# Tail of the second cross attention: one expert's low part, the bias rows' low part and the fourth weight load change their places

## The reference, cut to what matters

```python
x = x + tanh(g_xattn[1]) * xattn1(layernorm(x), ctx_1024, ...)    # 16 heads of 16
xs = layernorm(x).reshape(T, D)                                   # T = 800, D = 256
dist = sqrt(max(|xs|^2 + |centroid|^2 - 2 xs @ centroid.T, 1e-12))
w, sel = top_k(dist, 2); w = softmax(w)                           # 8 experts, 2 for each token
for e in range(8):
    h = silu(xs @ Wg[e] + bg[e]) * (xs @ W1[e] + b1[e])           # 684 hidden channels
    out = out + we[:, e:e+1] * (h @ W2[e] + b2[e])
x = x + tanh(g_ffn[1]) * out
```

## Time and profile before

| | us |
|---|---|
| median of three launches | 783.92 (783.83 to 784.07) |
| the profiled launch, its own time | 782.88 |
| span of the profiled launch | 781.1 |
| PE busy in it | 711.4 (91%) |
| DVE, ACT, POOL busy | 490.2, 379.0, 220.6 |

### The profile page before, as it was taken

The page is one execution under the profiler, slowest core; times in us unless marked ns, Lnnn a source line. Parts: engine busy times, 40 slices in busy tenths (PEclk is TensorE's granted clock), DMA queues, the critical chain, the costliest instruction groups (busy, mean ns, idle before and its releaser), DMA issues.

```text
span 781.1 us, 13394 instructions
## 1 busy us (share of the span) xinstructions
PE 711.4 (91%) x4735; PEld 596.4 (76%) x4735; DVE 490.2 (63%) x956; ACT 379.0 (49%) x820; POOL 220.6 (28%) x238
## 2 busy tenths in 40 slices
PE   6999999999989699998998999998993799999996
PEld 3578888889955588577995576676773699999995
DVE  3266666665328799466657667777777465666662
ACT  4513233323362289554434466565766165656561
POOL 0006765555400043600003411114000322334232
PEclk9999999999999899998999999999996699999999
DMA  6500000000072200000000878436052388999972
GB/s 231 233 1 21 20 20 20 20 1 1 1 293 100 79 3 1 1 1 1 0 11 33 179 175 193 116 98 183 25 213 85 111 299 279 331 298 325 302 217 60
DMA packets 31441, 89.45 MB, mean 115 GB/s; under 512 B 4201, under 2 KB 20841, under 8 KB 28049
## 3 DMA queue, kind: packets, MB, share of 16 engines
q1 hardware_dynamic: 27537, 83.36, 32.9%
q0 software_dynamic: 3840, 5.25, 3.3%
HBM read 74.74 MB, written 10.38 MB: 109 GB/s over the span
## 4 chain that ended last, share of the span: by engine, by line
PE 75%; DVE 14%; ACT 4%; issue 4%; DMA 3%; POOLq 0%; SPq 0%; DVEq 0%; ACTq 0%
PE PS L514 71%; DVE SM L2124 2%; PE PS L1096 2%; PE PS L685 1%; DMA XB<-token_rows,XROW 1%; DVE RB L1879 1%; DVE SM L1791 1%; DVE RQ L1881 1%; DVE PROD L1774 1%; PE PS L1066 1%; DVE KTHL L2086 1%; PE PS L913 1%; ACT SQ L1141 1%; DVE RW L1787 1%; ACT RO L1271 1%
## 5 line engine op out<-in xcount | busy, mean ns | idle before, releaser
L514 PE MATMUL PS<-CTXH,WKV0H 128*128 128x362 f32 x256 | 86.4, 338 | 3.8 <-DVE PROD L1774 3.2
L514 PE MATMUL PS<-CTXH,WKV0L 128*128 128x362 f32 x256 | 84.0, 328 | 0.0
L514 PE MATMUL PS<-CTXL,WKV0H 128*128 128x362 f32 x256 | 84.0, 328 | 0.0
L2124 DVE TENSOR_REDUCE SM<-PS 100x1 f32<-100x362 f32 x128 | 64.5, 529 | 30.5 <-PE PS L514 29.7
L1397 ACT ACTIVATE WK<-PS 120x400 f32<-120x400 f32 (+1 forms) x96 | 48.3, 508 | 39.9 <-PE PS L514 39.2
L1813 DVE TENSOR_TENSOR RW<-PS,RW 128x400 f32<-128x400 f32 x64 | 36.8, 574 | 47.4 <-ACT RW L1207 33.7
L1207 ACT COPY RW<-PS 128x361 f32<-128x361 f32 x64 | 29.6, 463 | 65.0 <-PE PS L514 52.5
L1670 POOL DMA_INDIRECT out<-YO,TROW x20 | 33.0, 1649 | 96.8 <-DMA out<-YO,TROW 69.5
L514 PEld LDWEIGHTS PS<-CTXH,WKV0H 128*128 128x128 f32 x256 | 48.1, 188 | 12.8 <-DVE PROD L1774 6.5
L514 PE MATMUL PS<-KST,QST 97*100 97x362 f32 x128 | 51.4, 412 | 5.4 <-DVE SM L2124 4.2
L514 PE MATMUL PS<-RB,HTT 114*128 114x256 f32 (+1 forms) x240 | 55.2, 379 | 0.6 <-ACT HTT L1509 0.6
(11 more groups left out here) (326 smaller groups left out, 1813.6 us busy)
## 6 DMA issues: line engine op xcount, KB each, us to landing
RB<-W SPq DMA_DIRECT2D x14, 1368.0 KB, 6.6
RB<-W SPq DMA_DIRECT2D x20, 768.0 KB
KST<-keys_by_head SPq DMA_DIRECT2D x24, 362.0 KB
RQ<-W SPq DMA_DIRECT2D x6, 1368.0 KB
keys_by_head<-KTHL SPq DMA_DIRECT2D x8, 724.0 KB, 3.6
CTX<-ctxT SPq DMA_DIRECT2D x16, 361.0 KB, 7.0
RB<-WK SPq DMA_DIRECT2D x16, 200.0 KB, 2.2
RW<-WGU SPq DMA_DIRECT2D x1, 2304.0 KB, 8.5
```

The lines of the kernel that those rows point to most:

```text
L514: return pe.matmul(out, lhsT, rhs, start=start, stop=stop)
L2124: dve.tensor_reduce(SM1[:, q % 2, j:j + 1], PS[0:S, i % 2, 0:KVE], AX_X, ALU.max, negate=True).then_inc(sem["c_maximum_found"], 1)
```

## The change

Four moves, none of which adds or removes an instruction of the engines or a transfer:

- DVE: `gu_low(0, 1)` goes from behind `route()` to a place behind `statistics(2)`, ahead of the wait for the last mix; `statistics(3)` and `statistics(4)` go ahead of that wait too.
- DVE: the bias rows' low part goes from behind `route()` into it, between WLOW and XROW, where DVE waits for the names' product.
- ACT: the bias rows' high part goes ahead of the square root.
- SP: `load_weights(3)` with its wait goes ahead of the rows' store and the residual's stores.

```diff
@@ sync
             load_down(0)
             load_down(1)
+            sp.wait_ge(sem["expert_weights_low_ready"], N0 + 2)
+            load_weights(3)
             sp.wait_ge(sem["rows_copied"], B)
             sp.dma_start(XROWS.rearrange("(b s) c -> s b c", s=S), ROWS[:, :, :]).then_inc(sem["rows_stored"], 16)
             sp.wait_ge(sem["c_aside_ready"], 2 + B)
...
-            sp.wait_ge(sem["expert_weights_low_ready"], N0 + 2)
-            load_weights(3)
@@ scalar
+            act.wait_ge(sem["moe1_small_loaded"], 64)
+            act.wait_ge(sem["zeros_set"], 7)
+            act.copy(BROWS[0:40, 0:2 * HID1], BRAW).then_inc(sem["bias_rows_ready"], 1)
             act.wait_ge(sem["router_scores_shifted"], 2)
             act.activation(FAR, pairs(TOPS), ACT.Sqrt).then_inc(sem["router_function_taken"], 1)
...
             act.preload_act_table_set("silu_and_others")
-            act.wait_ge(sem["moe1_small_loaded"], 64)
-            act.wait_ge(sem["zeros_set"], 7)
-            act.copy(BROWS[0:40, 0:2 * HID1], BRAW).then_inc(sem["bias_rows_ready"], 1)
@@ vector
             for b in (0, 1, 2):
                 statistics(b)
+            gu_low(0, 1)
+            for b in (3, 4):
+                statistics(b)
             dve.wait_ge(sem["c_heads_mixed"], 4 * B)
             place_sums(B - 1, sides(PS[:, 6, 0:4 * S]))
             pack_values(B - 1, sides(PS[:, 6, 0:4 * S]))
-            statistics(3)
             divide(B - 1)
-            for b in (4, 5, 6, 7):
+            for b in (5, 6, 7):
                 statistics(b)
...
                 link(dve.tensor_tensor(WLOW, WEIGHT, WHIGH[:, :], ALU.subtract))
+                dve.wait_ge(sem["bias_rows_ready"], 1)
+                dve.tensor_tensor(BROWS[32:40, :], BRAW[32:40], BROWS[32:40, :],
+                                  ALU.subtract).then_inc(sem["bias_rows_ready"], 1)
                 named = PS[:, 7, 64:64 + NBLK]
                 dve.wait_ge(sem["router_scores_summed"], 4)
...
             route()
-            gu_low(0, 1)
-            dve.wait_ge(sem["bias_rows_ready"], 1)
-            dve.tensor_tensor(BROWS[32:40, :], BRAW[32:40], BROWS[32:40, :],
-                              ALU.subtract).then_inc(sem["bias_rows_ready"], 1)
             tokens_low(0)
```

## The result

| | before | changed |
|---|---|---|
| median of three launches, us | 783.92 (783.83 to 784.07) | 777.34 (776.76 to 777.44) |
| ratio of the times | | 0.9918 (0.9891 to 0.9945) |
| the profiled launch, its own time | 782.88 | 777.34 |
| span of the profiled launch | 781.1 | 775.5 |

One launch of the kernel before, of the 98 on record, took 1,166 us at a mean clock of 0.56, and no figure here has it in. The rows that answer to those of before come first, then an account of where the time went.

A forecast was written before the change was run, and what follows sets the result against it. PE was taken to bound the kernel, idling 4.12 us for block 0's gather. The turn's 3.91 us plus edit 1's 0.79 made 4.70 us off 783.92: 779.2 us, own range 778.2 to 780.2, with cases 777.6 to 781.0.

The forecast's parts named there:

- Edit 1: DVE about the last mix: the second low half and two statistics fit into DVE's wait; gain 0.79 us, bounds 0.5 to 1.1.
- Edit 2: Bias rows' low part on DVE, between WLOW and XROW: shifts XROW and WEIGHED later, a loss of 0.2 us.
- Edit 3: Bias rows' high part on ACT, ahead of the square root: covered by the exponential's wait for DVE, cost nothing.
- Edit 4: Weights 3 on SP done near 590; block 0's gather lands before PE's product ends, the turn moving 3.91 us sooner.
- two readings: DVE's two-input subtraction holds up POOL's gather instruction (first), or making transfer descriptors is not held up by it (second).
- The sum at the turn: Turn of block 0's tokens on PE: 3.91 us plus edit 1's 0.79 us, 4.70 us sooner in all.
- Cases 2 and 4: Block 0's gather: 2: its 2.77 us are its own, 780.2 us, chance 0.18; 4: stores slow it, 783.3 us, 0.07.
- Case 3: PE's clock comes back earlier since PE works on without a gap: 1 us more gain, 778.2 us; chance 0.10.
- case 5: Slower: weights 3 ahead of the rows' store on SP delay that store and the gather, up to 785.8 us; chance 0.03.
- The clock: PE's half clock from the route into block 0: no change taken, though 2.1 us either way was possible; 1 us each side.

The follow-up runs named there:

- four buffers: The changed kernel with four YO buffers for the rows that go out, in place of two: median 779.30 us, ratio 0.9954.
- filler: The changed kernel with 58 unread products in PE's waits in the route: 779.34 us; with bias rows behind the route and four buffers as well: 777.10 us.

## Why the prediction was right and wrong

**Edit 1, forecast -0.79.** Right: -0.77 in the trace, and 0.72 the other way when the two statistics were put back.

**Edit 2, forecast +0.2.** The right sign, too small: +0.36 by the experiment. I had XROW behind BROWS at 603.30 to 603.41, so 0.12 to 0.23 us later, and let WEIGHED and PE's product shift by the same 0.2. In the trace BROWS put XROW 0.26 us later (15.75 us behind the statistics of batch 7, was 15.49), and WEIGHED another 0.13, which my sum had at nothing: 0.92 us after XROW, where it was 0.79.

**Edit 3, forecast 0.** Right. With the bias rows' low part put back, the only other edit in the route, XROW stands 19.31 - 3.79 = 15.52 us behind the statistics of batch 7, where it was 15.49 before.

**Edit 4, the turn 3.91 sooner, loss of edit 2 included.** Right in its parts. Weights 3 had moved but for the last 1% by 587, which is 588.4 in the old trace's times, where I had them done near 590; that only adds cover. The instruction took 1.39 us, by my working 604.66 + 1.0 - 604.46 = 1.2. The landing took at most 2.08, I had 2.0. PE's product became late next, as said. From the slot weights' product to the turn it is 3.44 us, where it was 7.73: I had counted the 3.60 us of that product in full, but the turn follows 0.16 us ahead of its modelled end.

The Trainium skill (SBUF — State Buffer, Who interferes with whom) left two readings. The runs side with the first: 2.77 and 2.76 us with GUL behind WEIGHED, 1.39 and 1.27 with only the last 0.32 and 0.2 us of WEIGHED beside its start. They don't show it to hold for every such subtraction: BROWS has two inputs in SBUF too, ran beside the gather from 601.38 on in the kernel with the bias rows put back, and held nothing up.

**The sum at the turn.** Forecast -4.70, measured -4.67, and the same distance (24.44) in four profiles, one of them with four buffers. That it fits to 0.03 us is luck: the slot weights' product began 0.38 us sooner where 0.59 were forecast, and the turn followed it 0.18 us sooner than forecast, so two errors of 0.2 us cancelled. Cases 2 and 4 are refuted by the kernels above. Case 3 came true in part in this launch (0.58 of its 1 us). The store that case 5 delays was issued at 592.37, 5 us after the engines had gone quiet, so it didn't occur.

**The step that failed** is "The clock": "I take no change ... and keep 1 us to each side for the range", and with it the last step, from the profiled launch to the median by a fixed 1.04 us. I had looked for the clock's part only in block 0, where it gave 0.58 us, within my 1 us and the way case 3 has it. But PE's clock falls to a half at places all over the span, and these differ from launch to launch: at 543 us before and not after, for 20 us at 349 in the second launch of before. Of the 6.6 us, 4.67 are the forecast sum; the 1.42 us from ahead of the mix and the 1.04 us between profiled launch and median, less 0.49 us given back behind the turn, are the rest, which the forecast had at nothing. A fit over 201 launches of 11 kernels, each with its own level and the time at half clock worked out from the mean clock, gives 0.42 us (+- 0.01) of time for each us at half clock. The last mix, which no kernel here changed, stood anywhere from 580.8 to 589.6 us. Pooled over three chips, 97 launches of before have a median of 783.7 us (8 in 10 of them from 781.8 to 786.0), and 17 of the changed kernel 778.9 (776.5 to 782.5): a difference of 4.9 us, near the forecast 4.7, with 3.8 to 6.5 as its interval by redrawing the launches. The traces say the same: from the last mix to the end of the span it took 197.97 and 198.72 us in the two of before, and 193.79, 193.13 and 193.53 in the three of the changed kernel, 4.9 us less in the mean. If three of each are drawn at random, their medians differ by over 6.3 us, which is out of my range, in 22 draws of 100; 8 in 10 give 2.9 to 7.2. The range was 3.4 us wide and should have been about 4.3 for this alone.

The failure was in the range, then, not in the mechanism. That the launches shown of before agreed within 0.24 us had made its median look far firmer than it is; the page of before had the warning in the 1.04 us between profiled launch and median, which I took for a constant.

**Open.** Why blocks come late in some launches (0 to 1.6 us in all) and whether four buffers end that, what decides where the clock falls in a launch, and why WEIGHED came 0.13 us later behind XROW.

## What to carry to other kernels

When work is moved beside an indirect gather, ask three things of the trace in turn: does its POOL instruction start beside a long subtraction on DVE, what else is in the DMA engines until it lands, and what does its reader do meanwhile; here one moved line gave 4.30 us of the 4.67 at the turn. Work put into a wait costs by how far it runs past the wait's end, and it becomes the wait as soon as what was waited for gets faster. Compare two launches by distances from an event that the edit can't reach, and take the scatter of whole launches from a dozen, not from three that agree.

## What the runs showed of the hardware

- The first gather's instruction ended 1.07 to 1.09 us behind the DVE instruction that ran beside its start, whichever that was: behind GUL before (605.95 to 607.03) and with weights 3 held (604.79 to 605.86), behind WEIGHED in the changed kernel (602.66 to 603.73) and with the bias rows put back (601.35 to 602.43). Later gathers that began 0.64 and 0.48 us into GUL (620.06 before, 613.19 changed) ended 0.83 and 0.81 us behind it, after 1.76 and 1.91 us; those of the first blocks with no GUL beside them took 0.94 to 0.97. GUL followed WEIGHED 0.09 us ahead of its end, and the hold went on; BROWS followed it 0.03 us behind its end, on 8 partitions in place of 128, and there was none. Which of the two differences matters was not tried. In both of the later gathers another GUL, on 128 partitions, began beside the instruction, 0.35 and 0.34 us behind the end of the first (621.34 before, 614.63 changed), and didn't hold it further.
- A load of 1,368 KB, issued 1.05 us ahead of the end of the gather's instruction, more than doubled the time from there to the landing of the gather's 128 KB: 5.16 us against 2.09 with the load held back.
- PE kept at work in the route ran the names' product in 2.08 us and the slot weights' product in 1.96, against 3.59 and 3.60: granted clocks of 1.00 and of 0.50, the two levels of 2.4 and 1.2 GHz. Yet the clock stood at 0.50 in block 0 in both kernels, behind a wait of 2.13 us ahead of the slot weights' product in the one, and waits of 0.42 and 0.95 us about it in the other. A longer filler there was not tried.
- The same program, launched 97 times, took 781 to 791 us. The time that PE spent at half clock accounts for 89% of the variance.
